# Routed rows split into a high and a low part as they are gathered, and both parts turned by fp32r products

## What is computed

```
topk_weight, topk_idx = _route(hidden, gate_weight, bias)      # 4 of 16 experts for each token
g = jnp.einsum('th,nfh->ntf', hidden, gate_w)                  # H = 256, F_MOE = 128
u = jnp.einsum('th,nfh->ntf', hidden, up_w)
act = jax.nn.silu(g) * u
routed = jnp.einsum('ntf,nhf,tn->th', act, down_w, weight_matrix)
out = routed + _swiglu(hidden, sh_gate_w, sh_up_w, sh_down_w)
```

## Time and profile before

| what | us |
|---|---|
| median of 3 runs | 859.78 |
| the profiled execution's own time | 855.01 |
| its span, first to last instruction | 853.3 |
| first row turned in the routed stage | 193.2 |
| end of the last down product of the routed stage | about 348 |
| mean granted TensorE clock | 0.948 |

### The profile page before, as it was taken

The page is one execution under the profiler, slowest core; times in us unless marked ns, Lnnn a source line. Parts: engine busy times, 40 slices in busy tenths (PEclk is TensorE's granted clock), DMA queues, the critical chain, the costliest instruction groups (busy, mean ns, idle before and its releaser), DMA issues.

```text
span 853.3 us, 14835 instructions
## 1 busy us (share of the span) xinstructions
PE 729.5 (85%) x5249; PEld 656.3 (77%) x5249; DVE 549.2 (64%) x1328; ACT 328.3 (38%) x680; POOL 464.0 (54%) x549
## 2 busy tenths in 40 slices
PE   4899989836778778238789999999999999999996
PEld 2344557736777778127789999999999999999996
DVE  4799977993445555348676767667666767654533
ACT  2221246612444445314454344444453343434321
POOL 4898963546455442336436636556475564543432
PEclk9899997967999999768899999999999999999999
DMA  8410014874555556342410201102011010000000
GB/s 257 152 38 12 26 37 122 186 157 160 147 152 144 139 146 123 106 139 77 127 35 25 65 1 57 32 13 63 13 32 57 1 50 27 1 14 1 2 13 13
DMA packets 42583, 63.16 MB, mean 74 GB/s; under 512 B 7152, under 2 KB 31760, under 8 KB 42512
## 3 DMA queue, kind: packets, MB, share of 16 engines
q1 hardware_dynamic: 34064, 38.71, 13.9%
q0 software_dynamic: 8352, 23.47, 12.3%
q10 hardware_dynamic: 96, 0.04, 0.0%
HBM read 47.37 MB, written 14.84 MB: 73 GB/s over the span
## 4 chain that ended last, share of the span: by engine, by line
PE 41%; DVE 6%; issue 4%; ACT 4%; POOL 3%; DMA 0%; POOLq 0%; ACTq 0%; DVEq 0%
PE bank L1387 15%; PE bank L1372 8%; PE bank L1419 6%; PE bank L1433 3%; PE bank L1405 3%; PE bank L1469 2%; DVE hid_lo L1883 2%; PE bank L1446 1%; ACT att_weights L1589 1%; POOL rows_back L1657 1%; DVE att_scaled L1793 1%; DVE am_lo L1872 1%; ACT am_hi L1574 1%; PE bank L1507 1%; ACT lora_w_hi L1550 1%
## 5 line engine op out<-in xcount | busy, mean ns | idle before, releaser
L1675 POOL TENSOR_TENSOR hid<-hid,rw_sb 128x256 f32<-128x256 f32 x112 | 90.7, 810 | 154.6 <-DVE hid L1877 154.4
L1387 PE MATMUL bank<-am_hi,lora_w_hi 128*128 128x256 f32 x448 | 126.9, 283 | 3.4 <-DVE am_lo L1872 3.4
L1877 DVE TENSOR_TENSOR hid<-hid,bank 128x256 f32<-128x256 f32 x112 | 46.7, 418 | 124.9 <-ACT hid L1557 124.2
L1387 PE MATMUL bank<-am_hi,lora_w_lo 128*128 128x256 f32 x448 | 126.7, 283 | 0.0
L1387 PE MATMUL bank<-am_lo,lora_w_hi 128*128 128x256 f32 x448 | 126.6, 283 | 0.0
L972 POOL DMA_INDIRECT rows_in<-y_scratch,slot_token x80 | 76.7, 958 | 76.5 <-DVE row_w L1173 44.6
L1557 ACT ACTIVATE hid<-bank 128x256 f32<-128x256 f32 x112 | 42.4, 385 | 183.3 <-PE bank L1387 170.7
L1387 PEld LDWEIGHTS bank<-am_hi,lora_w_hi 128*128 128x128 f32 x448 | 85.3, 190 | 3.6 <-POOL am_lo L1686 3.6
L1657 POOL DMA_INDIRECT rows_back<-slots_scratch,comb_idx x64 | 66.5, 1039 | 37.7 <-POOLq L666 22.2
L1387 PEld LDWEIGHTS bank<-am_hi,lora_w_lo 128*128 128x128 f32 x448 | 85.4, 191 | 0.0
L1387 PEld LDWEIGHTS bank<-am_lo,lora_w_hi 128*128 128x128 f32 x448 | 85.3, 190 | 0.0
(11 more groups left out here) (259 smaller groups left out, 2245.6 us busy)
## 6 DMA issues: line engine op xcount, KB each, us to landing
slots_scratch<-y_out SPq DMA_DIRECT2D x40, 256.0 KB
lora_stage_early<-in_lora_weights SPq DMA_DIRECT2D x16, 384.0 KB, 3.2
rows_in<-in_moe_weights SPq DMA_DIRECT2D x10, 384.0 KB, 3.9
moe_w_lo<-in_moe_weights POOLq DMA_DIRECT2D x10, 384.0 KB, 6.6
early_stage<-in_moe_weights SPq DMA_DIRECT2D x8, 384.0 KB, 7.5
x_sb<-in_x SPq DMA_DIRECT2D x4, 512.0 KB, 6.3
ctx_t<-in_ctx_t SPq DMA_DIRECT2D x4, 512.0 KB, 7.8
y_scratch<-y SPq DMA_DIRECT2D x8, 256.0 KB, 2.2
```

The source lines that it names most:

```text
L1387: last = nc.tensor.matmul(x_banks[F % 2][:, w * GT:(w + 1) * GT], wp, ap, start=False, stop=(half == 1 and k == 2), skip_group_check=True)
L1675: nc.gpsimd.tensor_tensor(f[:, F % 2, k, :], f[:, F % 2, k, :], rw_sb[:, F // FB % 2, k, :], ALU.mult)\
L1877: nc.vector.tensor_tensor(f[:, F % 2, k, :], f[:, F % 2, k, :], x_banks[F % 2][:, GT:2 * GT], ALU.mult)\
```

## The change

The rows are no longer turned as they were gathered. ACT first copies both tiles' rows to `row_hi` (fp32r), and DVE writes `row_lo`, the rest, to SBUF. TensorE then multiplies each part by an identity in fp32r (`ident_r`, made once by ACT): four products for the high part into one PSUM bank and four for the low part into the next of three banks. ACT copies the first bank to `xt_hi` and DVE copies the second to `xt_lo`; neither needs the other. A gather waits for `row_low`, `row_high` and `w_mul` in place of `turned` and `w_mul`, and TensorE no longer waits for `gathered`. The orders of ACT's and DVE's lists move as well.

```
+    with ExitStack() as place:
+        row_hi, row_lo = (place.enter_context(nc.sbuf_tensor(n, [P, 2, 2 * DIM], F32R)) for n in ("row_hi", "row_lo"))
+    ident_r = sb("ident_r", [P, P], F32R)
-    turn_banks, gu_banks, y_banks, ht_bank = banks[0:2], banks[2:4], banks[4:6], banks[6]
+    turn_banks, gu_banks, y_banks, ht_bank = (banks[0], banks[1], banks[7]), banks[2:4], banks[4:6], banks[6]
+        def turn_bank(q, part):
+            return turn_banks[(2 * q + part) % 3]
             def turn_rows(q):
-                pe.wait_ge(gathered[q % (ROW_SLOTS // 2)], 32 * (2 * q // ROW_SLOTS + 1))
-                if q >= 2:
-                    pe.wait_ge(xt_low, q - 1)
-                else:
+                if q == 0:
+                    pe.wait_ge(ident_cast, 1)
+                    pe.wait_ge(table_ready, 1)
                     pe.wait_ge(prod_done, SHARED_STEPS)
-                for c in range(HALVES):
-                    for k in range(2):
-                        last = nc.tensor.transpose(turn_banks[q % 2][:, (2 * c + k) * P:(2 * c + k + 1) * P],
-                                                   rows_in[:, (2 * q + k) % ROW_SLOTS, c * P:(c + 1) * P], ident[:, :])
-                last.then_inc(turned, 1)
+                for part, rows, ready in ((0, row_hi, row_high), (1, row_lo, row_low)):
+                    pe.wait_ge(ready, q + 1)
+                    if 2 * q + part >= 3:
+                        before = 2 * q + part - 3
+                        pe.wait_ge(xt_low if before % 2 else hi_done,
+                                   before // 2 + 1 if before % 2 else of_pairs(before // 2 + 1))
+                    for c in range(HALVES):
+                        for k in range(2):
+                            last = nc.tensor.matmul(turn_bank(q, part)[:, (2 * c + k) * P:(2 * c + k + 1) * P],
+                                                    rows[:, q % 2, k * DIM + c * P:k * DIM + (c + 1) * P], ident_r[:, :],
+                                                    start=True, stop=True)
+                    last.then_inc(turned, 1)
...
+            def split_rows(q):
+                act_eng.wait_ge(gathered[q % (ROW_SLOTS // 2)], 32 * (2 * q // ROW_SLOTS + 1))
...
+                if q >= 2:
+                    act_eng.wait_ge(turned, 2 * (q - 1) - 1)
+                slot0 = 2 * q % ROW_SLOTS
+                nc.scalar.copy(row_hi[:, q % 2, :].rearrange("p (k d) -> p k d", k=2),
+                               rows_in[:, slot0:slot0 + 2, 0:DIM]).then_inc(row_high, 1)
...
-                nc.scalar.copy(xt_hi[:, q % 2, :], turn_banks[q % 2][:, :]).then_inc(hi_done, 1)
+                nc.scalar.copy(xt_hi[:, q % 2, :], turn_bank(q, 0)[:, :]).then_inc(hi_done, 1)
...
-                    pool.wait_ge(turned, (i - ROW_SLOTS) // 2 + 1)
+                    pool.wait_ge(row_low, (i - ROW_SLOTS) // 2 + 1)
+                    pool.wait_ge(row_high, (i - ROW_SLOTS) // 2 + 1)
                     pool.wait_ge(w_mul, (i - ROW_SLOTS) // 2 + 1)
...
+            def split_rows(q):
+                dve.wait_ge(row_high, q + 1)
+                if q >= 2:
+                    dve.wait_ge(turned, 2 * (q - 1))
+                slot0 = 2 * q % ROW_SLOTS
+                nc.vector.tensor_tensor(row_lo[:, q % 2, :].rearrange("p (k d) -> p k d", k=2),
+                                        rows_in[:, slot0:slot0 + 2, 0:DIM],
+                                        row_hi[:, q % 2, :].bitcast(FP32).rearrange("p (k d) -> p k d", k=2),
+                                        ALU.subtract).then_inc(row_low, 1)
...
-                nc.vector.tensor_tensor(xt_lo[:, q % 2, :], turn_banks[q % 2][:, :],
-                                        xt_hi[:, q % 2, :].bitcast(FP32), ALU.subtract).then_inc(xt_low, 1)
+                nc.vector.tensor_copy(xt_lo[:, q % 2, :], turn_bank(q, 1)[:, :]).then_inc(xt_low, 1)
```

More of the change, by code:

```diff
@@ L683, in moe_phase @@
             "h_turned", "ht_high", "ht_low", "y_copied", "ctx_loaded"))
-        lora_staged = sem("lora_staged_early")
+        lora_staged, row_high, row_low, ident_cast = map(sem, ("lora_staged_early", "row_high", "row_low", "ident_cast"))
         block = s.enter_context(nc.Block())
@@ L817, in gate_up @@
                 pe.wait_ge(xt_low, q + 1)
+                pe.wait_ge(hi_done, of_pairs(q + 1))
                 if q >= 2:
@@ L898, in hidden_high @@
                 nc.scalar.copy(ht_hi[:, q % 2, :], ht_bank[:, (q % 2) * DIM:(q % 2 + 1) * DIM]).then_inc(ht_high, 1)
+            def split_rows(q):
+                act_eng.wait_ge(gathered[q % (ROW_SLOTS // 2)], 32 * (2 * q // ROW_SLOTS + 1))
+                if q == 0:
+                    act_eng.wait_ge(prod_done, SHARED_STEPS)
+                if q >= 2:
[3 more added lines that the diff above has]
+                               rows_in[:, slot0:slot0 + 2, 0:DIM]).then_inc(row_high, 1)
             def rows_high(q):
-                act_eng.wait_ge(turned, q + 1)
+                act_eng.wait_ge(turned, 2 * q + 1)
                 if q >= 2:
                     act_eng.wait_ge(gu_done, of_pairs(q - 1) - SHARED_EARLY)
-                else:
-                    act_eng.wait_ge(down_done, SHARED_STEPS)
-                nc.scalar.copy(xt_hi[:, q % 2, :], turn_banks[q % 2][:, :]).then_inc(hi_done, 1)
+                nc.scalar.copy(xt_hi[:, q % 2, :], turn_bank(q, 0)[:, :]).then_inc(hi_done, 1)
             def y_copy(q):
@@ L920, in gate_silu @@
                   .then_inc(silu_done, 1)
+            act_eng.wait_ge(order_done, 4)
+            nc.scalar.copy(ident_r[:, :], ident[:, :]).then_inc(ident_cast, 1)
+            split_rows(0)
             for n in range(STEPS_ROUTED):
+                if n < ROUTED_PAIRS:
+                    rows_high(n)
                 if 3 <= n < ROUTED_PAIRS + 3:
                     hidden_high(n - 3)
-                if n < ROUTED_PAIRS:
-                    rows_high(n)
+                if n + 1 < ROUTED_PAIRS:
+                    split_rows(n + 1)
                 if n >= 4:
@@ L1178, in slot_weights @@
                 nc.vector.reduce_sum(slot_w[:, q % 2, :], row_w[:, q % 2, :, :], axis=AX.X).then_inc(w_found, 1)
+            def split_rows(q):
[7 more added lines that the diff above has]
+                                        ALU.subtract).then_inc(row_low, 1)
             def rows_low(q):
-                dve.wait_ge(hi_done, of_pairs(q + 1))
+                dve.wait_ge(turned, 2 * q + 2)
                 if q >= 2:
                     dve.wait_ge(gu_done, of_pairs(q - 1) - SHARED_EARLY)
-                nc.vector.tensor_tensor(xt_lo[:, q % 2, :], turn_banks[q % 2][:, :],
-                                        xt_hi[:, q % 2, :].bitcast(FP32), ALU.subtract).then_inc(xt_low, 1)
+                nc.vector.tensor_copy(xt_lo[:, q % 2, :], turn_bank(q, 1)[:, :]).then_inc(xt_low, 1)
             def hidden(q):
@@ L1197, in hidden @@
                 last.then_inc(prod_done, 1)
+            split_rows(0)
             for n in range(STEPS_ROUTED):
+                if n < ROUTED_PAIRS:
+                    rows_low(n)
                 if 3 <= n < ROUTED_PAIRS + 3:
@@ L1203, in _ @@
                     weight_products(n)
-                    rows_low(n)
+                if n + 1 < ROUTED_PAIRS:
+                    split_rows(n + 1)
+                if n < ROUTED_PAIRS:
                     slot_weights(n)
```

## The result

The changed kernel takes 849.47 us (median of 4 runs, 846.49 to 853.2), the kernel before on the same chip 860.33 us (4 runs): a ratio of 0.9866, 95% interval 0.9827 to 0.9906. It is 1.3% faster. The prediction had said 871.9 us and slower. The profiled execution took 849.35 us, its span is 847.6.

A forecast was written before the change was run, and what follows sets the result against it. The routed stage's middle was taken as bound by a 7.45 us two-pair loop with the hold, not TensorE's work. Terms 9.4 + 1.3 + 1.4 = +12.1 us give 867.1 profiled, plus 4.8 for the median: 871.9 us; range 845 to 892.

The forecast's parts named there:

- I lean to it staying: Routed stage: the hold would survive, since gate_up instructions still take their address from a register; forecast case, chance 0.38.
- The hold: Routed stage: TensorE's finished work reaches others late while POOL issues four gathers; its last part is 0.98 us.
- the period of two pairs: Routed stage's middle: a loop from release through row_w and four gathers to the next release, 7.45 us.
- the last of its conditions: POOL's gathers: w_mul, raised behind hidden_low as before, still comes last, so releasing a slot earlier brings nothing.
- The order term: ACT's list: rows_high ahead of hidden_high adds 0.59 us per two pairs, 16 x 0.59 = 9.4 us.
- The holds go: Rival for the routed stage: without removed waits and reads it runs at TensorE's 3.25 us a pair; 845.9 us, chance 0.30.
- The price of a product: TensorE's turn: each 128-column fp32r product costs 0.113 us, upper bound 0.216, making a pair 3.25 us.
- ACT and DVE: Added copies and subtraction: ACT's pair rises to 2.35 us, DVE's to 2.6 to 2.8, both below TensorE's 3.25.
- Start and end: Routed stage's edges: splits before the first turn +1.3 us, three pairs in the last window +1.4 us.

The follow-up runs named there:

- h3: Kernel before with only the change's new order of the ACT and DVE lists, on a chip with the hold: 853.38 us, ratio 0.9928.
- h4: Kernel after with the ACT and DVE lists back in the order of before, on a chip with the hold: 864.22 us, ratio 1.0066.
- i2: Kernel before with one move: DVE makes weight_products(n) behind rows_low(n) instead of ahead of it: 859.12 us, ratio 0.9964.
- f2: Kernel after with the gathers of two pairs waiting for the second pair's signals, so four are issued in a row: 872.48 us, ratio 1.0138.
- g1: Kernel before with only the new order of the ACT and DVE lists, on the chip without the hold: 845.19 us, ratio 1.0245.
- e1 to e4: Kernel before, gathers waiting for xt_low, not turned; kernel after, turned wait added; kernel after, gathered wait added; kernel before, transposing an ACT copy: ratios 0.9991, 0.9919, 0.9905, 1.0053.
- h1: Kernel before, unchanged, run again on a chip with the hold: 859.81 us, ratio 1.0011.
- i1: Kernel before with two small POOL multiplications behind each pair of gathers, on a chip with the hold: 838.7 us, ratio 0.9743.
- f4: Kernel before with one small POOL multiplication behind each pair of gathers: 859.1 us, ratio 0.9982.
- g2: Kernel after with the ACT and DVE lists in the order of before, on the chip without the hold: 840.34 us, ratio 1.0207.
- g4: Kernel before with two small POOL multiplications behind each pair of gathers, on the chip without the hold: 834.18 us, ratio 1.0135.

## Why the prediction was wrong

*The step that failed* is the one that ends "I lean to it staying". The hold is real and POOL's gathers make it, as the prediction said. But it asked what the gathers, the waits and the tiles have to do with each other, and not whether the gathers would still come in fours. I carried the period of two pairs over as a fact of the kernel; on the chips with the hold it hangs on the order of two lists (h3, h4), and the change alters that order. In its place the runs show gathers in twos: 31 waits of POOL in the middle window for 16, and a SiLU 0.17 us behind its matmul for 1.90. With the two lists put back as they were (h4) the fours and a lag of 1.63 us return, and the kernel takes 864.22 us. A hint was in my own working: `w_mul`, "the last of its conditions", was not raised "as before" but had got behind a copy that waits for the turn of the same step. By i2 this move alone does not make the twos.

*The order term* (+0.59 in a period of two pairs) was a cost that exists and was put on the wrong loop. f2, with fours, took 872.48 us against my 871.9, which looks like a proof of the sum for fours and is in part luck. Its two pairs take 8.23 us (gathers from 251.49 to 259.72) where I had 8.04: the four gathers last 5.15, not 4.73, since one of them takes 1.37, and the gap is 3.08 where my sum makes it 2.72 + 0.59 = 3.31. Its gathers also wait for the signals of a later pair, which my kernel's did not. Without the hold the order costs 0.66 us a pair (g1), more than I said; with the hold it takes 6.8 us off the whole kernel (h3). A term of the cost was the cure.

*"The holds go"* came out 3.6 us from the measured 849.47 (845.9), for a reason that falls, and so by luck: no wait or reading that was taken away matters (e1 to e4). Its test, a SiLU within 0.1 us of its matmul, was nearly met at 0.17. Its remark that the parallel copies help to keep the pace fits the runs: h3, which lacks them, needs 3.45 us a pair. They were not tried alone.

*The price of a product* was right. Four of them take 0.61 us with 0.28 for one alone, (0.61 - 0.28) / 3 = 0.11; I had taken 0.113, and TensorE's pair of 3.25 us is as predicted to the hundredth. One product thus costs what one transpose costs (0.109); the turn is dearer because it takes eight, 0.93 us from 254.39 to 255.32, where four transposes took 0.44. The Trainium skill ("Perfetto Trace Analysis", section "Transposes") has a logical transpose done as a transpose and not as a matmul. The trace agrees in that the turn got dearer, but this did not decide the time: TensorE had 0.98 us a pair to spare.

*ACT and DVE*: 78.56 us busy in 34.7 pairs are 2.26 us a pair (2.35 predicted), 84.74 are 2.44 (2.6 to 2.8).

*Start and end.* The stage's last down product starts at 341.19 us. From there to the end of the span (847.6) are 506.4 us. In h1, the kernel before, the last one starts at 350.56 and the span ends at 856.9, which are 506.3. So all of the gain lies in the routed stage. The start was dearer than the 1.3 us I gave it: the first turn is at 195.68, not 193.2, and the first window ran at a granted clock of 0.66, not 0.78. The clock of two stretches of it, in the columns of the earlier trace rows:

```profile
199.00:203.00 4.00, 3.71 (x17) 3.71 (x18) 2.27 (x6) 1.34 (x3) 2.50 (x3) 0.50 0.44 118
...
207.00:211.60 4.60, 4.60 (x42) 4.60 (x42) 3.58 (x12) 2.15 (x5) 2.89 (x4) 1.00 0.24 64
```

```profile
195.68 1.09 PE L823 MATMUL bank<-ident_r,row_hi 128*128 128x128 f32 x4 [8.01 <-ACT row_hi L922]
...
207.19 0.64 PE L823 MATMUL bank<-ident_r,row_hi 128*128 128x128 f32 x4
```

Four products take 1.09 us there and 0.64 later. The first turns come behind 8.01 us of waiting, and up to 203 us the clock is at 0.50, its lower level of 1.2 GHz; from 207 it is 1.00. In the kernel before it is 1.00 from 203 on.

## What to carry to other kernels

When an engine's finished work is seen late while another issues its gathers, look at how these are spread before asking what waits for what: here a rest of 0.9 us behind every two gathers was worth 2.6% on a chip with the hold (and cost 1.3% on the one without), and twice the work on the turn paid for itself only because it came with such a rhythm. A period that spans two steps can hang on the order of the lists, so a change that moves a list must be asked whether the period survives it. And a gain of this size may belong to the chip: take the kernel before along on every chip, and compare only inside one.

## What the hardware showed that I had not expected

- POOL's indirect gathers, issued in a row, delay the moment at which ACT sees TensorE's matmuls as finished: lags mostly of 1.4 to 3.4 us in fours (before, h1, f2, h4), 0.55 in h3's twos, 0.38 in i1 (gap 0.94), 0.17 in the kernel after (gap 1.03). On the kernel before, a gap of 0.59 us brought no gain (f4) and one of 0.94 brought 2.6% (i1). What carries the delay stays open: no row names it ("remote").
- The gap alone does not set the lag: h3's is longer than that of the kernel after, and so is its lag. What the two share is the SiLU's distance from the end of the second gather, 257.13 - 256.39 = 0.74 us in the kernel after and 261.83 - 261.15 = 0.68 in h3. The matmuls end 0.57 and 0.13 us behind that gather, and the lag is what is left. In the pairs of the kernel after in which the matmul ends 0.8 us or more behind that gather, the lag is 0.04.
- Whether it happens depends on the chip. It showed on the four chips of the groups e, f, h and i, with medians of 859 to 862 us for the kernel before, and not on the one of group g, with 824.37 us. The same kernel, g2 and h4, took 840.34 and 864.22; the one with the rest, g4 and i1, 834.18 and 838.7.
- The sign of the change probably goes with it. On the chip without the hold the order alone costs 2.5% (g1) and the rest of the change 2.1% (g2). The whole change was not run there; TensorE's 3.25 us a pair in g2 makes me expect about g2's 840 us, 2% slower than before. That is an estimate, and the one thing I would measure next.
